# The bias row of the values: added to each value tile behind its projection, or to each token tile behind its softmax

## The reference, cut to what matters

```python
xn = layernorm(x)
# attention, one head of 512
n = layernorm(xn) * gamma + beta
q, k, v = n @ qkv[:, :512], n @ qkv[:, 512:1024], n @ qkv[:, 1024:]
a = softmax(causal(q @ k.T / sqrt(512)))
s = (a @ v) @ o_proj + xn            # residual
g = silu(mixture_of_experts(xn))
out = x + s * g
```

## Time and profile before

| What | Value |
|---|---|
| median of 3 runs | 1150.11 us (1149.41 to 1152.07) |
| profiled execution | 1149.77 us |
| its span in the trace | 1148.0 us |
| TensorE busy | 1131.4 us |
| VectorE, ScalarE, POOL busy | 572.4, 473.5, 423.6 us |
| mean granted clock of TensorE | 0.997 of full speed |

### The profile page before, as it was taken

The page is one execution under the profiler, slowest core; times in us unless marked ns, Lnnn a source line. Parts: engine busy times, 40 slices in busy tenths (PEclk is TensorE's granted clock), DMA queues, the critical chain, the costliest instruction groups (busy, mean ns, idle before and its releaser), DMA issues. The chain is left out here.

```text
span 1148.0 us, 21220 instructions
## 1 busy us (share of the span) xinstructions
PE 1131.4 (99%) x6598; PEld 627.4 (55%) x6599; DVE 572.4 (50%) x1236; ACT 473.5 (41%) x859; POOL 423.6 (37%) x656
## 2 busy tenths in 40 slices
PE   8999999999999999999999999999999999999997
PEld 5555555555556555555555555554454454444454
DVE  6876666677469331222111221112477377367467
ACT  5544344435332232333223232234654645555643
POOL 1333233332400222222222222212755754764763
PEclk9999999999999999999999999999999999999999
DMA  9899999989533599999997777776876777766364
GB/s 277 221 238 215 239 239 224 220 212 239 137 76 67 131 191 206 208 202 203 204 190 197 178 184 175 172 177 152 168 184 171 166 160 189 152 161 184 109 156 120
DMA packets 365003, 209.31 MB, mean 182 GB/s; under 512 B 304308, under 2 KB 314816, under 8 KB 364936
## 3 DMA queue, kind: packets, MB, share of 16 engines
q1 hardware_dynamic: 354104, 172.76, 64.7%
q0 software_dynamic: 10800, 35.69, 12.6%
q10 hardware_dynamic: 32, 0.02, 0.0%
HBM read 89.44 MB, written 46.01 MB: 118 GB/s over the span
## 5 line engine op out<-in xcount | busy, mean ns | idle before, releaser
L706 PE MATMUL pair<-arena 128*128 (+2 forms) x3240 | 506.2, 313 | 2.9 <-DMA arena<-arena 2.7
L706 PEld LDWEIGHTS pair<-arena 128*128 128x128 f16 x3240 | 316.0, 98 | 185.6 <-DMA arena<-arena 3.2
L1647 DVE SCALAR_TENSOR_TENSOR arena<-pair,slot_unit,arena 128x352 f32<-128x352 f32 x71 | 41.5, 584 | 269.1 <-ACT arena L1537 212.6
L713 PE MATMUL bank<-arena 128*128 x639 | 149.3, 379 | 0.0
L1537 ACT ACTIVATE arena<-pair,slot_unit 128x352 f32<-128x352 f32 x71 | 39.3, 554 | 205.4 <-PE pair L706 178.5
L1251 POOL COPY arena<-token_of 128x1 uint32 (+1 forms) x71 | 12.9, 181 | 265.2 <-issue 103.1
L1941 PE MATMUL pair<-arena 128*128 128x512 f16 (+3 forms) x576 | 98.0, 326 | 1.3 <-ACT arena L2009 1.2
L713 PEld LDWEIGHTS bank<-arena 128*128 128x128 f16 x639 | 62.5, 98 | 66.2
L1954 PE MATMUL bank<-arena 128*128 128x512 f16 x411 | 93.5, 379 | 0.0
L1253 POOL DMA_INDIRECT arena<-xn_rows,arena x71 | 71.7, 1010 | 55.6 <-POOL arena L1251 54.0
L1921 PE MATMUL bank<-arena 128*128 128x512 f16 x384 | 86.1, 379 | 0.0
(11 more groups left out here) (205 smaller groups left out, 1360.3 us busy)
## 6 DMA issues: line engine op xcount, KB each, us to landing
slot_rows<-arena SPq DMA_DIRECT2D x71, 256.0 KB
arena<-in_L_attn_x_dram SPq DMA_DIRECT2D x64, 256.0 KB, 3.5
xn_rows<-arena SPq DMA_DIRECT2D x32, 260.0 KB, 2.6
shared_rows<-arena SPq DMA_DIRECT2D x32, 256.0 KB
arena<-shared_rows SPq DMA_DIRECT2D x32, 256.0 KB
out_dram<-arena SPq DMA_DIRECT2D x31, 256.0 KB, 2.8
arena<-in_L_ffn_wg_dram SPq DMA_DIRECT2D x32, 176.0 KB, 3.1
arena<-in_L_ffn_wu_dram SPq DMA_DIRECT2D x32, 176.0 KB, 3.3
```

What stands on the lines that cost most here:

```text
L706: last = pe.matmul(bank[:, 0:width], xt[:, a, c, :], weights(c, b, col, width), start=(c == 0 and i == 0), stop=(c == KC - 1 and i == 2))
L713: last = pe.matmul(bank[:, :], ht[:, a, c, :], weights(c, b), start=(start and c == 0 and i == 0), stop=(stop and c == HC - 1 and i == 2))
L1647: v.scalar_tensor_tensor(sbuf[u], u_banks[u][:, 0:H], slot_unit[u][:, 1:2], sbuf[u], ALU.mult, ALU.mult).then_inc(slot_h_ready, 1)
```

## The change

The bias row is no longer added to each of the 32 token rows. Each of the 32 value groups is now first written by VectorE as an f32 row `zv`, bank * scale + `bias_rows` (`proj_shift`). ScalarE's high part is a copy of `zv`, and VectorE's low part is `zv` less the high part. There are two buffers `zv`; the semaphore `s_shifted` goes, `v_shifted` comes. `combine` and `combine_last` wait for `xn_made` in place of `s_shifted`.

```diff
@@ buffers and semaphores
+            for u in range(2):
+                c["zv", u], at = carve(at, [D], F32)
-            s_shifted = sem("s_shifted")
+            v_shifted = sem("v_shifted")
+            def zv_free(g_):
+                return g_ - 1 if g_ % KC >= 2 else g_ - KC - 1
@@ ScalarE
                 def proj_high(b, g_):
                     is_v, h, n = proj_group(g_)
-                    act.wait_ge(proj_done, b * PG + g_ + 1)
                     if is_v:
-                        nc.scalar.activation(proj_target(g_, 0), proj_bank(g_)[:, :], ACT.Copy,
-                                             scale=Q_SCALE).then_inc(proj_hi, 1)
+                        act.wait_ge(v_shifted, b * QT + h * TH + n + 1)
+                        nc.scalar.copy(proj_target(g_, 0), c["zv", n % 2]).then_inc(proj_hi, 1)
                     else:
+                        act.wait_ge(proj_done, b * PG + g_ + 1)
@@ VectorE
+                def proj_shift(b, g_):
+                    is_v, h, n = proj_group(g_)
+                    if is_v:
+                        dve.wait_ge(proj_done, b * PG + g_ + 1)
+                        wait(dve, proj_lo, b * PG + zv_free(g_))
+                        v.scalar_tensor_tensor(c["zv", n % 2], proj_bank(g_)[:, :], Q_SCALE, bias_rows,
+                                               ALU.mult, ALU.add).then_inc(v_shifted, 1)
+
                 def proj_low(b, g_):
                     is_v, h, n = proj_group(g_)
                     dve.wait_ge(proj_hi, b * PG + g_ + 1)
                     if is_v:
-                        v.scalar_tensor_tensor(proj_target(g_, 1), proj_bank(g_)[:, :], Q_SCALE, proj_target(g_, 0),
-                                               ALU.mult, ALU.subtract).then_inc(proj_lo, 1)
+                        v.tensor_tensor(proj_target(g_, 1), c["zv", n % 2], proj_target(g_, 0), ALU.subtract
+                                        ).then_inc(proj_lo, 1)
@@ VectorE, combine_first
                     v.reciprocal(c["inv", u], sums[:, t % 4:t % 4 + 1]).then_inc(inv_ready, 1)
-                    dve.wait_ge(xn_made, t + 1)
-                    v.tensor_tensor(row, row, bias_rows, ALU.add).then_inc(s_shifted, 1)
@@ VectorE, combine and combine_last
-                    dve.wait_ge(s_shifted, t + 1)
+                    dve.wait_ge(xn_made, t + 1)
@@ VectorE, the projection groups
+                        proj_shift(b, g_)
                         proj_low(b, g_)
```

More of the change, by code:

```diff
@@ L2107, in combine_first @@
                 def combine_first(t):
-                    u, row = t % 2, c["s", t % S_AHEAD]
+                    u = t % 2
                     dve.wait_ge(exp_done, t + 1)
                     v.reciprocal(c["inv", u], sums[:, t % 4:t % 4 + 1]).then_inc(inv_ready, 1)
-                    dve.wait_ge(xn_made, t + 1)
-                    v.tensor_tensor(row, row, bias_rows, ALU.add).then_inc(s_shifted, 1)
                 def combine(t):
```

## The result

| | before | changed |
|---|---|---|
| median, 7 runs each | 1150.62 us (1149.07 to 1152.93) | 1157.49 us (1154.0 to 1161.18) |
| ratio of the changed kernel | | 1.0057, 95% interval 1.0042 to 1.0073 |
| profiled execution, its span | 1149.77, 1148.0 us | 1161.18, 1159.4 us |

The changed kernel is slower by 6.6 us (1150.6 times 0.0057, interval 4.8 to 8.4). A second series, with six runs of it, gave 1.0053 (1.0041 to 1.0065). The forecast was 1155.4, slower by 5.3.

A forecast was written before the change was run, and what follows sets the result against it. TensorE, busy 99% of the span, was taken as the bound: waits of 1.55 + 1.55 + 1.5 + 2.3 = 6.9 us over four batches, less 1.6 at the end, gave +5.3, so 1155.4 us (range 1151.2 to 1158.6).

The forecast's parts named there:

- What bounds: Whole kernel: TensorE busy 99% of the span, so other engines' steps cost only where it waits; VectorE totals mislead.
- Prices: Attention stage: 32 VectorE shifts at 0.75 us added (23.9), 32 bias adds at 0.89 removed (28.5); copy 0.62, split 0.69.
- Place 1: Value groups 12 and 13, ahead of a batch's first scores: longer chain and POOL's turn make TensorE wait 1.65 us.
- Place 2: Groups 14 and 15 inside the first tiles' softmax: soften(0) to soften(1) about 5.05 to 5.2 us, exponentials 1.4 to 1.5 later.
- The sum by batch: Both places overlap, so each batch pays about the larger: 1.55, 1.55, 1.5 and 2.3, together 6.9 us.
- worse: Rival, whole stage: delays add up as late ScalarE work hits further splits; +8.2 us, 1158.3 or more; chance 0.09.
- The end: Last product and after: bias adds gone from VectorE's way, 1.1 us, and POOL's residual add 0.45 earlier; together -1.6 us.
- Total: Whole kernel: 6.9 less 1.6 gives +5.3 us, predicted median 1155.4.
- Less turn-taking: Rival, at the value splits: POOL doesn't get in between VectorE's instructions; +3.4 us, 1153.5; chance 0.20.
- Faster: Rival, at both places: the value chain is hidden, only the end's gain remains; 1148.5 us; chance 0.09.

The follow-up runs named there:

- F: Changed kernel with POOL's two adds of mix cut to 8 of 512 columns; ratio to the kernel before 0.9975.
- G: Kernel before with POOL's two adds of mix cut to 8 of 512 columns; ratio to the kernel before 0.9988.
- A: Changed kernel with end(2) on VectorE moved from behind group 12 to behind group 13; ratio to the kernel before 1.0041.
- H: Changed kernel with each of POOL's two adds of mix replaced by a memset of a scratch row; ratio to the kernel before 0.9987.
- J: C with soften(0) on VectorE also put ahead of the split of group 14; ratio to the kernel before 0.9976.
- D: Kernel before with the 32 bias adds left out, so the bias is nowhere in the result; ratio to the kernel before 0.9978.
- C: Changed kernel with both the move of A and the move of B; ratio to the kernel before 0.9982.
- K: J with begin(4) behind group 14's copy and, in the last batch, group 15 back in its first place; ratio to the kernel before 0.9976.
- E: Changed kernel with the 32 bias adds kept as well, so the bias is added twice; ratio to the kernel before 1.0065.
- B: Changed kernel with group 15's shift, copy and split moved behind soften(1), p_high(1) and p_low(1); ratio to the kernel before 1.0036.

## Why the prediction was right, and where it missed

**What bounds.** Right. VectorE's total was no guide: F has the added chain and costs nothing against G, and VectorE is at 50% in both kernels.

**Prices.** The shift is 683 ns in the median (677 to 693 over 32), against my 0.75; it is nearer the 691 of L2077 than the 746 of L2121. So the VectorE work that the change adds is 22 us and not 24. The copy and the undisturbed split are 0.62 and 0.69 as told.

**Place 1.** Right in mechanism and order, POOL's turn between split(12) and end(2) included. Size: in batches 1 to 3 the first scores start 46.23 us into the batch for 44.68 before, so 1.55 us later for my 1.65; the idle time shown is 1.40, 1.38 and 1.39, since matmul records overlap at their ends. Batch 0 had 2.10 for 1.55: end(2), and POOL's add with it, came 0.8 us later in its batch than before. A, F and H show the cause on the chip.

**Place 2.** The distance is right in batches 1 to 3, 4.9 us for 5.05; in batch 0 it was 5.96 and 6.31. The price is right where it can be seen alone: batch 2 of A is 1.37 us longer than before, for my 1.5. But that price came from a batch whose first softmax was late already, and I took it for the price of the distance, as the expectations for F and G show. F, H and J show that the first softmax has to be late too. In the kernel before it was late in batches 1 and 2 by ScalarE's waits for a gathered row (3.6 and 2.8 us). In the changed kernel these waits are 0.6 us or less, and in batches 1 to 3 split(14) meets POOL's add instead and takes 0.84, 2.01 and 1.57 us (first profile).

**The sum by batch.** Told 1.55, 1.55, 1.5, 2.3; measured, second profile less before, 3.70, 1.42, 1.32, 2.95. Batch 0 has 1.7 us in it that the sum had no term for: TensorE's clock. In batch 3 the step that was too small is soften(0): told at 1093.9, which is 48.6 us into the batch, it came at 49.24, because split(14) met POOL's add (1.57 us for 0.69). With it the scores of tile 4 came 2.78 us later than before, for the 2.3 told. Further on, combine's product with g and end(t) each met POOL once more (L2137 and L2118 at 1121.44 and 1123.13, 1.77 and 1.75 us). Both are the "worse" rival at one point.

**The end.** The 1.1 us of the tail came exactly (7.30 to 6.21). The 0.45 us of POOL's add came too (1.72 to 1.27), but the last product still waited 1.43 us, so nothing of it was seen; in D it was worth more. Not counted were 1.3 us from VectorE's last instruction to the end of the span. It is 3.54 in all four kernels with the adds and 2.2 to 2.6 in all without. The sum took VectorE for the engine that ends last, and it is POOL: in the four kernels with the adds, and in D, F and H, the end is its DRAIN, 5.41 us behind its last add, which starts 3.5 us after the start of the last product with the adds and 1.3 to 2.3 us after it without. What the DRAIN does in this time no run shows.

**Total.** 3.70 + 1.42 + 1.32 + 2.95 - 1.09 - 1.33 = 7.0 us by the traces, of which 1.7 is the clock, and 6.1 to 6.6 by the timed runs, for my 5.3. The terms that were mis-sized are batch 0 and batch 3, both too small, and the end, too small as well. So the number is partly luck: without the clock the batches cost 7.7 us for my 6.9, and the end gave 2.4 for my 1.6, and the two misses of 0.8 cancel.

**Rivals.** "Less turn-taking" fell: end(2) took 1.76, 1.75 and 1.75 us in batches 1 to 3, not 1.09. "Faster" needed the two places to have slack, and C, J and K are just that kernel.

A rule of the Trainium skill, "SBUF — State Buffer", section "SBUF: two separate sides", has whoever starts first hold the shared pair of ports. Twice more, at 826.64 in the changed kernel (2.10 us) and at 1091.57 in C (2.28 us), VectorE's instruction shows the earlier start and lost, so that rule does not tell who waits here. The Trainium skill also says there that a VectorE instruction with two SBUF inputs collides only with a POOL instruction that reads SBUF. H agrees: 0.68 to 0.70 us beside a memset.

## What to carry to other kernels

When work moves from one place on an engine to another, compare the chains and not the totals: 28 us of adds taken off VectorE were worth 2.5 us (D), and 22 us put on it cost 8 to 9 us against D in one order (the changed kernel) and, within the noise, nothing in another (C). A hand-over to another engine and back (VectorE, ScalarE, VectorE) blocks all that is queued behind it, so put behind it only what nobody waits for. Ahead of such a chain look for what reads only SBUF on VectorE while POOL reads SBUF too; the meetings shown here made 0.69 us into anything from 0.84 to 2.36, and the shifts, which read a bank, stayed at 0.68 to 0.69 throughout. And see which engine ends last: here the last add of an engine that was idle 63% of the time set the end.

## What the runs showed of the hardware

**TensorE's clock fell after a wait in the middle of the kernel.** Stretches of the changed kernel around the first scores of batch 0 (columns as above; the clock is the third number from the end):

```profile
828.00:830.00 2.00, 0.68 (x4) 0.10 (x1) 1.34 (x2) 0.62 (x2) 1.85 (x3) 1.00 0.48 127
830.00:832.00 2.00, 1.22 (x8) 0.97 (x9) 1.29 (x2) 2.00 (x4) 1.18 (x2) 0.80 0.90 241
832.00:834.00 2.00, 2.00 (x9) 1.10 (x8) 1.39 (x3) 1.54 (x2) 1.90 (x2) 0.50 0.66 150
834.00:836.00 2.00, 2.00 (x10) 0.81 (x8) 0.90 (x3) 0.97 (x3) 1.86 (x3) 0.85 0.33 113
```

TensorE stood for 2.10 us, went on, and then the granted clock was 0.50 (1.2 in place of 2.4 GHz) for some 3 us. The matmuls of this kernel there, and below them those of E, where the clock stayed at 1.00:

```profile
830.78 2.38 PE L1947 MATMUL pair<-arena 128*128 128x256 f16 x12 [2.10 <-DVE arena L2091]
832.95 3.57 PE L1927 MATMUL bank<-arena 128*128 128x512 f16 x12
```

```profile
827.29 1.49 PE L1948 MATMUL pair<-arena 128*128 128x256 f16 x12 [1.85 <-DVE arena L2092]
828.62 2.75 PE L1928 MATMUL bank<-arena 128*128 128x512 f16 x12
```

The same two rows of matmuls took 0.9 and 0.8 us longer in the changed kernel than in E. The fall came in the three profiles where that wait was 1.96, 2.10 and 2.29 us (both of the changed kernel, and B), and in none with shorter waits (1.85 in E and, at an exponential, in A; under 1.5 everywhere else in the stage). So this stall cost nearly twice its length. It need not come in every execution: one run of the changed kernel in each series has a mean granted clock of 1.000, which the fall alone would bring to 0.999 or less.

**Writes alone don't collide.** POOL's memsets of 1.43 us left VectorE's 128x512 instructions with two SBUF inputs at 0.68 to 0.70 us in all 57 meetings of H with a memset and no add; POOL's adds of 1.27 stretched them to as much as 2.36 (split(12) in batch 0 of B).

**POOL's closing DRAIN.** It ended 5.41 us after the end of POOL's last residual add in all fourteen profiles, and set the end of the span in seven of them.
